# Cross-attention on one core: half of the keys' low-weight product moved next to the scores, and the turns of context and x moved ahead of the turn of the probabilities

## The reference

```python
h = _layernorm(x, gamma, beta)
Q = (h @ Wq).reshape(B, NQ, N_HEADS, HEAD_DIM)
K = (context @ Wk).reshape(B, NC, N_HEADS, HEAD_DIM)
V = (context @ Wv).reshape(B, NC, N_HEADS, HEAD_DIM)
attn = jnp.einsum('bihd,bjhd->bhij', Q, K)
attn = jax.nn.softmax(attn, axis=-1) * scale
vals = jnp.einsum('bhij,bjhd->bihd', attn, V).reshape(B, NQ, INNER)
out = vals @ Wo + bo
x = x + out
```

## Time and profile before

| what | before |
|---|---|
| median of 3 runs | 364.79 (364.53 to 364.8) |
| the profiled execution | 364.5 |
| its span, first to last instruction | 362.6 |
| PE, PEld busy in the span | 97%, 84% |
| ACT, DVE, POOL busy in the span | 70%, 67%, 45% |
| mean granted TensorE clock | 0.999 |

### The profile page before, as it was taken

How to read it: one execution, slowest core, us unless ns; L and a number is a source line. 1 busy time by engine, 2 the same in 40 slices (tenths; PEclk the granted TensorE clock), 3 DMA queues, 4 the chain that set the end, 5 groups by cost and what they waited for, 6 DMA issues and landing times.

```text
span 362.6 us, 8915 instructions
## 1 busy us (share of the span) xinstructions
PE 353.0 (97%) x3116; PEld 305.8 (84%) x3116; DVE 242.9 (67%) x534; ACT 252.1 (70%) x762; POOL 164.5 (45%) x321
## 2 busy tenths in 40 slices
PE   5999999999999999999999999999999999999986
PEld 5779888888888888988888988888988888988865
DVE  5887566866568666686667675686565866566654
ACT  4898876766677766777766776766677766677762
POOL 5677884335444262444532464323744325344321
PEclk9999999999999999999999999999999999999999
DMA  6930010200002000020000100020000000000000
GB/s 191 272 118 3 1 52 2 82 0 3 2 0 82 0 0 0 0 80 0 1 0 29 51 0 0 0 78 1 0 0 0 29 2 0 2 2 31 3 0 31
DMA packets 10743, 10.39 MB, mean 29 GB/s; under 512 B 960, under 2 KB 10176, under 8 KB 10720
## 3 DMA queue, kind: packets, MB, share of 16 engines
q1 hardware_dynamic: 10192, 9.64, 8.6%
q10 hardware_dynamic: 416, 0.33, 0.3%
q0 software_dynamic: 112, 0.13, 0.2%
HBM read 8.00 MB, written 2.10 MB: 28 GB/s over the span
## 4 chain that ended last, share of the span: by engine, by line
PE 92%; ACT 3%; DVE 3%; DMA 1%; issue 0%; POOL 0%; DVEq 0%
PE mix_ps L710 16%; PE st_ps L805 15%; PE st_ps L688 13%; PE o_ps L777 12%; PE w_ps L752 12%; PE w_ps L730 12%; PE w_ps L823 10%; ACT prob L405 2%; DMA x_in<-in_x_dram 1%; PE w_ps L671 1%; PE w_ps L663 1%; ACT qk_hi L415 0%; DVE w_lo L480 0%; DVE neg_max L563 0%; DVE qk_lo L576 0%
## 5 line engine op out<-in xcount | busy, mean ns | idle before, releaser
L316 POOL TENSOR_SCALAR prob<-prob,inv 128x256 f32<-128x256 f32 x256 | 120.1, 485 | 158.0 <-DVE inv L570 157.6
L405 ACT ACTIVATE prob<-st_ps,neg_max 128x256 f32<-128x256 f32 x256 | 118.0, 473 | 27.0 <-DVE neg_max L563 27.0
L563 DVE TENSOR_REDUCE neg_max<-st_ps 128x2 f32<-128x512 f32 x128 | 82.5, 683 | 35.2 <-PE st_ps L688 34.9
L458 ACT ACTIVATE prob_t<-st_ps 128x512 f32<-128x512 f32 x64 | 38.4, 600 | 44.2 <-PE st_ps L805 44.2
L638 DVE COPY prob_t<-st_ps 128x512 f32<-128x512 f32 x64 | 44.1, 691 | 28.6 <-PE st_ps L805 25.2
L710 PE MATMUL mix_ps<-prob_t,v_sb 128*64 128x256 f32 x504 | 61.5, 385 | 0.1
L805 PE MATMUL st_ps<-ident,prob 128*128 128x128 f32 x512 | 61.1, 272 | 0.0
L805 PEld LDWEIGHTS st_ps<-ident,prob 128*128 128x128 f32 x512 | 56.7, 141 | 0.1
L576 DVE TENSOR_TENSOR qk_lo<-w_ps,qk_hi 128x512 fp32r<-128x512 f32 x62 | 42.8, 690 | 20.6 <-ACT qk_hi L415 20.6
L405 ACT ACTIVATION_READ_ACCUMULATOR prob<-st_ps,neg_max 128x1 f32 x256 | 52.7, 206 | 0.0
L710 PEld LDWEIGHTS mix_ps<-prob_t,v_sb 128*64 128x64 f32 x504 | 33.4, 136 | 17.9 <-issue 0.3
(11 more groups left out here) (121 smaller groups left out, 589.1 us busy)
## 6 DMA issues: line engine op xcount, KB each, us to landing
x_in<-in_x_dram SPq DMA_DIRECT2D x8, 256.0 KB, 3.1
out_dram<-y_sb SPq DMA_DIRECT2D x7, 256.0 KB, 2.2
c_in<-in_ctx_dram SPq DMA_DIRECT2D x7, 192.0 KB, 2.9
w_raw<-in_L_xattn_Wq_dram SPq DMA_DIRECT2D x8, 128.0 KB, 3.3
w_raw<-in_L_xattn_Wo_dram SPq DMA_DIRECT2D x4, 256.0 KB, 3.5
w_raw<-in_L_xattn_Wk_dram SPq DMA_DIRECT2D x4, 128.0 KB, 4.0
w_raw<-in_L_xattn_Wk_dram SPq DMA_DIRECT2D x8, 64.0 KB, 3.6
w_raw<-in_L_xattn_Wv_dram SPq DMA_DIRECT2D x2, 256.0 KB, 3.5
```

What stands on the lines that cost most here:

```text
L316: last = nc.gpsimd.tensor_scalar(prob[:, e, r, :], prob[:, e, r, :], inv[:, e, r:r + 1], SCALE, ALU.mult, ALU.mult)
L405: last = nc.scalar.activation(prob[:, e, r, :], st_ps[e][:, r * ROWS:(r + 1) * ROWS], ACT.Exp, bias=neg_max[:, e, r:r + 1], accum_out=sums ...
L458: nc.scalar.activation(prob_t[:, e, :, :].rearrange("p a b -> p (a b)"), st_ps[e][:, :], ACT.Copy)\
L563: nc.vector.tensor_reduce(neg_max[:, e, :], st_ps[e][:, :].rearrange("p (r j) -> p r j", r=RT), AX, ALU.max, negate=True).then_inc(max_rea ...
```

## The change

The last pass of the keys (`w_lo` of tile K0+1 against slot 1 of `c_t`, whose lower half is low part by low part) is taken out of `keys` for all pairs that the scores use from step 2 on. In its place a new function `keys_rest` multiplies only the 64 rows of the high part, by row halves: pair 0 on partitions 0 to 63, for which a copy of the high part is kept in a new tile `c_rest`, pair 1 on partitions 64 to 127, into two banks. It stands between `scores` and `mix`, and starts the sums in `w0_ps` and `w1_ps`. The waits that stood in front of the two `keys` (for the values' copy `v_ready`, for the readers of `w1_ps`) stand in front of it.

`turn_c` (from sequence 2 on) and `turn_x` move from the end of the step to the place between `output` and `turn`, in the same steps 4b-4 and 4b-3, and wait there for `qk_lo_ready` of the same step. Their readers move with them into the same step: on ACT in front of the `prob_t` copies, with one copy more for `c_rest`; on DVE `context_lo` in front of the `prob_t` copies; the norm of x moves to the end of step 4b-4, and the statistics to the step before that, 4b-5. TensorE's program is written out as a straight line, with no loop.

```diff
+        c_rest = sb("c_rest", [HALF, 2, ROWS], fp32r)
-        LOAD, STATS, TURN_C, NORM, SPLIT_C, SPLIT_H, PUT = -5, -4, -4, -3, -3, -2, PER_SEQ + 1
+        LOAD, STATS, TURN_C, TURN_X, SPLIT_H, PUT = -5, -5, -4, -3, -2, PER_SEQ + 1
...
             def context_hi(b, ps):
                 nc.scalar.activation(c_t[:, b % 2, 0, :], ps[:, 0:ROWS], ACT.Copy)
+                nc.scalar.activation(c_rest[:, b % 2, :], ps[HALF:P, ROWS:2 * ROWS], ACT.Copy)
                 nc.scalar.activation(c_t[HALF:P, b % 2, 1, :], ps[HALF:P, ROWS:2 * ROWS], ACT.Copy)\
                     .then_inc(c_hi_ready, 1)
...
-            def keys(t, a, turns, parts=(0, 1)):
+            def keys(t, a, parts=(0, 1)):
...
+                shared = t >= 2 * BATCH
                 passes = context_products(K0)
+                if shared:
+                    passes = passes[:-1]
...
+            def keys_rest(u):
+                b, p = divmod(BATCH * (u + 1), PAIRS)
+                pe.wait_ge(v_ready, 1 if u == 1 else u + 1)
...
+                pe.wait_ge(qk_lo_ready, BATCH * (u + 1))
...
+                high = (c_rest[:, b % 2, :], c_t[HALF:P, b % 2, 1, :])
+                for a in range(BATCH):
+                    own = slice(a * HALF, (a + 1) * HALF)
+                    nc.tensor.matmul(qk_banks(u)[a][:, 0:ROWS],
+                                     w_lo[own, K0 + 1, (p + a) * P:(p + a + 1) * P], high[a],
+                                     start=True, stop=False, skip_group_check=True)
...
-            def step(u, turns):
+            def step(u):
                 if 0 <= u < STEPS:
-                    scores(u, turns)
+                    scores(u)
+                if 1 <= u < STEPS - 1:
+                    keys_rest(u)
                 if 1 <= u <= STEPS:
-                    mix(u - 1, turns)
+                    mix(u - 1)
...
+                b = of_seq(u, TURN_C, 2)
+                if b is not None:
+                    pe.wait_ge(c_loaded[b % 2], 16 * (b // 2 + 1))
+                    pe.wait_ge(qk_lo_ready, BATCH * u + HEADS)
+                    turn_c(b, context_bank(b))
+                b = of_seq(u, TURN_X, 1)
+                if b is not None:
+                    pe.wait_ge(x_norm_ready, b + 1)
+                    pe.wait_ge(qk_lo_ready, BATCH * u + HEADS)
+                    turn_x((w1_ps, w1_ps), ROWS)
                 if 0 <= u < STEPS:
-                    turn(u, turns)
+                    turn(u)
                 if 1 <= u < STEPS - 1:
-                    values(u + 1, turns)
-                b = of_seq(u, TURN_C, 1)
-                if b is not None:
-                    pe.wait_ge(c_loaded[b % 2], 16 * (b // 2 + 1) + turns(16))
-                    pe.wait_ge(qk_lo_ready, BATCH * u + HEADS + turns(16))
-                    turn_c(b, context_bank(b))
-                b = of_seq(u, NORM, 1)
-                if b is not None:
-                    pe.wait_ge(x_norm_ready, b + 1 + turns(2))
-                    pe.wait_ge(qk_lo_ready, BATCH * u + HEADS + turns(16))
-                    turn_x((w1_ps, w1_ps), ROWS)
...
-            walk(pe, step, 2)
+            for u in range(-1, LAST):
+                step(u)
```

More of the change, by code:

```diff
@@ L308, in step @@
                     weight_lo(14)
-                b = of_seq(u, NORM, 1)
+                b = 1 if u == 1 else of_seq(u, TURN_C, 2)
                 if b is not None:
@@ L389, in step @@
                     values_out(u, w0_ps)
[L390 to L399 removed]
+                if u == 1:
+                    act.wait_ge(c_turned, 2)
+                    context_hi(1, context_bank(1))
                 def probabilities(e):
@@ L451, in step @@
                     weight_hi(16)
+                b = of_seq(u, TURN_C, 2)
+                if b is not None:
+                    act.wait_ge(c_turned, b + 1 + turns(2))
+                    context_hi(b, context_bank(b))
+                b = of_seq(u, TURN_X, 1)
+                if b is not None:
+                    act.wait_ge(h_lo_ready, DT * b + turns(4))
+                    act.wait_ge(x_turned, b + 1 + turns(2))
+                    hidden(b, w1_ps)
                 if 0 <= u < STEPS:
@@ L583, in step @@
                 maximum(1)
-                b = of_seq(u, SPLIT_C, 1)
-                if b is not None:
-                    context_lo(b, context_bank(b), turns)
+                if u == 1:
+                    context_lo(1, context_bank(1), turns)
                 maximum(2)
@@ L627, in step @@
                     weight_lo(16)
-                if b is not None and b >= 2:
-                    dve.wait_ge(x_turned, b + turns(2))
-                    norm(b, turns)
+                b = of_seq(u, TURN_C, 2)
+                if b is not None:
+                    context_lo(b, context_bank(b), turns)
                 if 0 <= u < STEPS:
@@ L641, in step @@
                             weight_lo(13)
+                b = of_seq(u, TURN_C, 2)
+                if b is not None:
+                    dve.wait_ge(x_turned, b + turns(2))
+                    norm(b, turns)
                 b = of_seq(u, STATS, 2)
@@ L693, in scores, with mix @@
                                     last.then_inc(scores_made, 1)
-            def mix(w, turns):
-                pe.wait_ge(v_ready, RT * (w // RT) + RT + turns(8))
+            def mix(w):
+                pe.wait_ge(v_ready, RT * (w // RT) + RT)
                 if w >= 1:
-                    pe.wait_ge(mix_lo_ready, w + turns(8))
+                    pe.wait_ge(mix_lo_ready, w)
                 for a in range(BATCH):
                     for h in range(2):
-                        pe.wait_ge(prob_t_ready[h], BATCH * w + a + 1 + turns(16))
+                        pe.wait_ge(prob_t_ready[h], BATCH * w + a + 1)
                     p = (BATCH * w + a) % GROUP
@@ L730, in keys, with queries @@
                         nc.tensor.matmul(ps[:, 0:ROWS], w[:, i, cols], c_t[:, b % 2, k, :],
-                                         start=w is w_hi and i == K0 and k == 0,
-                                         stop=w is w_lo and i == K0 + 1, skip_group_check=True)
-            def queries(t, a, turns):
+                                         start=not shared and w is w_hi and i == K0 and k == 0,
+                                         stop=w is passes[-1][0] and i == passes[-1][1],
+                                         skip_group_check=True)
+            def keys_rest(u):
+                b, p = divmod(BATCH * (u + 1), PAIRS)
+                pe.wait_ge(v_ready, 1 if u == 1 else u + 1)
+                if u == 1:
+                    pe.wait_ge(v_ready, RT)
+                seq = of_seq(u - 1, TURN_C, 2)
+                if seq is not None:
+                    pe.wait_ge(c_lo_ready, seq + 1)
+                seq = of_seq(u - 1, TURN_X, 1)
+                if seq is not None:
+                    pe.wait_ge(h_full_ready, DT * seq + 1)
+                pe.wait_ge(qk_lo_ready, BATCH * (u + 1))
+                if p == 0:
+                    pe.wait_ge(c_lo_ready, b + 1)
+                if BATCH * (u + 1) in FOR_K:
+                    low_ready(pe, FOR_K[BATCH * (u + 1)])
+                high = (c_rest[:, b % 2, :], c_t[HALF:P, b % 2, 1, :])
[4 more added lines that the diff above has]
+                                     start=True, stop=False, skip_group_check=True)
+            def queries(t, a):
                 b, p = divmod(t, PAIRS)
@@ L744, in queries @@
                 elif p == 0:
-                    pe.wait_ge(h_lo_ready, DT * b + DT + turns(4))
+                    pe.wait_ge(h_lo_ready, DT * b + DT)
                 for n, (w, h) in enumerate(((w_hi, h_hi), (w_lo, h_hi), (w_hi, h_lo))):
@@ L756, in queries, with output @@
                 last.then_inc(projected, 1)
-            def output(w, turns):
+            def output(w):
                 b, s = divmod(w, PER_SEQ)
@@ L767, in output @@
                 elif s == 0:
-                    pe.wait_ge(y_ready, b + turns(2))
-                pe.wait_ge(mix_lo_ready, w + 1 + turns(8))
+                    pe.wait_ge(y_ready, b)
+                pe.wait_ge(mix_lo_ready, w + 1)
                 for a in range(BATCH):
@@ L798, in last_output, with turn @@
                             last.then_inc(o_added, 1)
-            def turn(u, turns):
+            def turn(u):
                 for e in range(HEADS):
-                    pe.wait_ge(scaled, HEADS * u + e + 1 + turns(32))
+                    pe.wait_ge(scaled, HEADS * u + e + 1)
                     for r in range(RT):
@@ L808, in turn, with values @@
                     last.then_inc(turned, 1)
-            def values(n, turns):
+            def values(n):
                 g, j = divmod(n, RT)
@@ L816, in values @@
                     high_ready(pe, FOR_V[g])
-                pe.wait_ge(qk_lo_ready, n + 1 if n < RT else BATCH * n + 1 + turns(16))
+                pe.wait_ge(qk_lo_ready, n + 1 if n < RT else BATCH * n + 1)
                 passes = context_products(V0)
@@ L850, in step @@
```

(4 more changed lines are left out.)

35 lines of the change are left out of this document (20 added, 15 removed).

## The result

The changed kernel takes 372.64 (372.41 to 372.71, 6 runs) against 364.80 (364.53 to 364.82, 6 runs): ratio 1.0215, interval 1.0202 to 1.0228, so 7.8 slower. Forecast were 371.3 and a range of 367.0 to 374.5. The profiled execution took 372.41 with a span of 370.6, 8.0 more than before, at a mean clock of 1.00.

A forecast was written before the change was run, and what follows sets the result against it. PE was taken to bound the kernel, with 92% of the chain of waits. Six sequences +6.5, step 1 +0.84 and steps 2, 3, 28, 29, 30 -0.60 gave +6.8 on 364.5: 371.3, range 367.0 to 374.5.

The forecast's parts named there:

- The matmuls: Keys in steps 1 to 30: two full matmuls out, one 64-row pair in, net 0.12 a step saved, 3.6 together.
- The short stall: Moved transposes of context and x wait on PE for `qk_lo` of pair 1: 0.36, with the restart 0.47.
- Steps 4b-4: Steps turning the context (b = 2 to 7): stall, then scores waiting for head 1's copy; 11.45 against 11.07, +0.38.
- Steps 4b-3: Steps turning x: DVE late, first maximum at 1.81, transposes stall 0.96 (1.07 with restart); 12.02 against 11.07, +0.95.
- Step 1: Turns x too; PE waits for `qk_lo`: 0.85 + 0.11, less the 0.12 saved, +0.84.
- Only the short stall: Rival: DVE makes up its lateness before the first maximum; the whole +3.0, 367.5; chance 0.14.
- Faster: Rival: stalls hidden, 3.6 saving left, 360.9; decides at a mean stall of 0.28 in 13 turning steps; chance 0.07.
- the halves do not run side by side: Rival: the two half matmuls run in a row, 30 x 0.12 more, 374.9; chance 0.06, further waits included.
- The clock: Rival: TensorE falls to 1.2 GHz over long stall and twenty transposes; 7 steps x 2.7 = 19, 390; chance 0.02.

The follow-up runs named there:

- e8: e1 with both new 64-row matmuls on the same row half (partitions 0 to 63, both with `c_rest`): 365.46.
- e1: The changed kernel with `turn_c` (sequence 2 on) and `turn_x` (sequence 1 on) writing `mix_ps` instead of `w1_ps`: 362.65.
- e6: The changed kernel with ACT's copy into `c_rest` taken from SBUF and put behind its `prob_t` copies: 370.11.
- e3: The changed kernel with DVE's `y_sb` moved from in front of the first maximum to behind the second one: 369.37.
- e2: The changed kernel without the pair of 64-row matmuls and without `c_rest` and its copy; transposes and readers stay moved: 371.67.
- e7: The changed kernel with the edits of e1 and e6 together: 361.59.
- e4: The kernel before, TensorE in a straight line, with the 64-row pair behind the mix and `c_rest` copied; transposes and readers not moved: 367.34.

## Why the prediction was right

**The matmuls**: -0.12 a plain step was forecast and is measured (10.63 to 10.51), except in step 2, where nothing is saved; e8 shows that it hangs on the row halves.

**The short stall**: 0.47 forecast, 0.47 measured in step 12. Its parts came out otherwise: from DVE's end (152.62 + 0.69 = 153.31) to PE's start it was 0.15, not the 0.05 of the earlier trace rows, while the restart behind it cost 0.02 (four transposes in 0.46 and not 0.44), not 0.11. The mechanism was right; that the two errors cancel is luck. e1 shows the wait to be the cause.

**Steps 4b-4**: +0.38 forecast, +0.53 measured. Here the term was too small: I had the copy of head 1 done at 11.3, 0.1 before PE wanted it, and entered 0.03 for this wait (11.45 against 11.42). It ends at 156.22 + 0.69 = 156.91, just when PE would go on, and with the 0.15 from DVE to PE the scores start at 157.06. Without the third copy (e6) the step takes the 11.45 that I had forecast with it.

**Steps 4b-3**: +0.95 forecast, +0.92 measured; the first maximum at 1.73 where 1.81 was worked out, the stall 1.00 where it was 0.96. e3 shows that the extra over the short stall is DVE's lateness, and e1 that it matters only through the wait.

**Step 1**: +0.84 forecast, +0.86 measured. **The start**: I counted nothing, and it costs 0.38 (step 1 starts at 21.97 against 21.59). The third copy stands on the path from the first context to the first keys: DVE's first subtraction of the context, before and after,

```profile
7.04 0.42 DVE L509 TENSOR_TENSOR c_t<-st_ps,c_t 128x256 fp32r<-128x256 f32 x1
```

```profile
7.40 0.42 DVE L515 TENSOR_TENSOR c_t<-st_ps,c_t 128x256 fp32r<-128x256 f32 x1 [0.29 <-ACT c_t L358]
```

I priced the copy where the kernel repeats itself and overlooked the one place where every engine waits in a row. That term was missing; the one that was most too small is that of steps 4b-4.

Together 6 x 0.53 + 6 x 0.92 + 0.86 + 0.38 - 16 x 0.12 = 8.0, as the span has it. The forecast was 6.8: it lacked 0.9 in steps 4b-4, 0.4 at the start and 0.1 in step 2, and had 0.2 too much in steps 4b-3.

**The rivals.** "Only the short stall" is what e3 comes near to (369.4), and it needs an edit. "Faster" needed stalls under 0.28; they are 0.47 and 1.00. That the halves do not run side by side is answered by their starts, at most 0.03 apart in steps 12 and 13, and by e8. The clock did not fall: over the stretch with the long stall and twenty transposes the granted clock (the third number from the end) stays at 1.00, 2.4 GHz, and the sixteen behind the stall take 1.66 (166.06 to 167.72), as those behind the short one do (153.92 to 155.59):

```profile
164.40:169.10 4.70, 3.86 (x30) 3.20 (x29) 2.10 (x4) 2.31 (x5) 0.93 (x2) 1.00 0.00 0
```

The first line of the earlier trace rows, on which this rival was given little, was misread. It prints 1.00 for 3.70 to 7.90, but the transposes in it are slow at first; PE before:

```profile
5.11 1.06 PE L663 MATMUL st_ps<-ident,c_in 128*128 128x128 f32 x4
5.96 1.38 PE L658 MATMUL o_ps<-ident 128*128 128x128 f32 x6
```

Four take 0.85 here, where four cost 0.44 in a step. So TensorE stood at its lower level, 1.2 GHz; the trace's record of the clock begins 7.1 into the span, and the row counts what lies ahead of it as 1.00. From there it was at 2.4 GHz, and it had done nothing but transposes before it rose. The rule of the Trainium skill ("TensorE: Matmul & The Clock Gate", Part 4: PE-mode transpose) that transposes do not count as activity is not borne out by this rise.

**What the sum hid.** The 3.6 that the pair saves was entered in full, and the stall reckoned with PE coming 0.12 earlier. The two cancel in 13 of the 30 steps: there PE goes on when `qk_lo` is done, however early it comes. The pair was worth 1.9 in this kernel, less than its third copy cost, and e2 missed because I used 3.6 again.

## What to carry to other kernels

When work is moved to an earlier place on the engine that sets the time, look at who last reads the buffer it writes, and compare that reader's end with the new start: here 7.83 against 7.52 in the step made the short stall, and the readers that moved along made it twice as long in the next step; together they turned 3.6 of saving into 7.8 of loss. Ask for another buffer that has been read by the new time: with it the same moves cost almost nothing (e1, e7). Matmuls taken out in front of a wait save nothing; count them only in the stretches that do not wait, and price a new instruction at the start of the program as well as in its steady steps.

## What the runs showed of the hardware that was not expected

A pair of 64-row matmuls costs 0.12 among others of its form and 0.31 between 64-column and full matmuls (e4), so the form that follows must be counted with it. The change from scores to mix has 0.09 of its own (0.21 against 0.12), with or without the pair. From the mix to the pair takes as long as from the mix to full matmuls: 1.88 from the start of the mix in both (167.13 to 169.01 in e4, 147.20 to 149.08 in the changed kernel). The Trainium skill ("TensorEngine Tiling (Array Packing)", Key Properties) says that changing the tiling mode drains TensorE. It gives no price; the 0.19 by which 0.31 exceeds 0.12 would be one if the drain is its cause, which no run here separates.

TensorE starts this program at its lower clock, 1.2 GHz (transposes 0.21 apart, 0.11 in the steps), and when it rises differs between executions, though all begin with the same transposes: the records of the clock begin between 6.9 (e6) and 9.7 (e2) into the span in the ten traces. Why it differs no run shows.
